# Graph attention by lists of edges: an index beyond a bound for edges of a later block

## The chip, the cores and the metric

The kernel runs on one core of a Trainium2 chip. The metric is the device time of one execution in microseconds (us): 4299.35 us, the median of three runs (4293.27, 4299.35 and 4299.38).

## What is computed

The program is a network of four graph layers and four feed-forward layers over 3125 nodes with 256 features and 50000 edges (src, dst), sorted by dst. The change touches the first two graph layers, which are graph attention with 4 heads of 64 features. Cut to what matters:

```
h = (x @ W.T).reshape(N, 4, 64)
e = leaky_relu(a_s[src] + a_d[dst], 0.2)          # one number per edge and head
m = segment_max(e, dst);  p = exp(e - m[dst])
alpha = p / (segment_sum(p, dst)[dst] + 1e-16)
out = segment_sum(alpha[:, :, None] * h[src], dst)
```

In the first layer every node also has an edge to itself. The other layers (mixtures of experts, a recurrence, graph convolutions, a dense form of the third attention) are not touched.

## The kernel before

**Blocks and places.** The nodes are cut into T = 25 blocks of P = 125. Since the edges are sorted by dst, the edges of a block are a run of the list. The list lies in HBM as a table (`k.EP`) with W = 17 edges to a row, four numbers to an edge: dst, two codes for another purpose, and src. Block b reads 128 rows of it, beginning at or just before its first edge (the number is in `k.at`), so partition p holds 17 successive edges, and a block has 128 x 17 = 2176 places. A block has 2000 edges in the mean. The places left over hold edges of the block before (fewer than two rows of them) and, mostly, edges of the block after. Places beyond the last edge hold -1.

**The edge loop.** `by_edges` runs once for each of the two layers (call them loop 1 and loop 2), 25 blocks each, and all engines work on several blocks at a time, in step by semaphores:

- SyncE loads the records of a block (`records`, L842) into one of six buffers `egs`.
- VectorE makes the indices, `indices(b)` at L894 to L899: src as an int32, not below 0, into one of three buffers `ids`. It first waits for the records and, from block 3 on, for the gathers of block b - 3, which read the same buffer.
- GpSimd (POOL in the profile) gathers, L826 to L834: for each of the 17 columns w one indirect DMA, which fetches for each of the 128 partitions the row of `k.HR` (264 floats: features with a one per head, and the source term of the score) that the index names. The rows land in one of four buffers `hgs`. It waits for the indices, and from block 4 on for the sums of block b - 4, which used the buffer last.
- VectorE, when the 17 gathers of block b have landed, copies the source terms for the list of maxima (`spread`, L947 and L948), and in later steps makes the maxima, the scores (`logits`) and the weights, and multiplies the gathered rows by them (`weigh`, L1008). Places whose dst is not in the block get weight 0, by the column of ones that their empty row of the one-hot matrix leaves out.
- TensorE sums the rows of a block by a matmul with the one-hot matrix of dst (L1156); ScalarE copies, widens and takes exponentials.

Beside this every second block, in each loop, also makes a block of a dense count matrix for the later layers (class `Adjacency`): VectorE at L545 and L556, TensorE at L619 and L630, ScalarE at L567, L580, L586 and L596.

**The order on VectorE** is written out by hand: step i holds maxima(i-2), sums(i-3), spread(i-1), indices(i+1), logits(i-2), the close of block i-3, the work for the count matrix, weigh(i-2) and hot(i). The indices of block i+1 are made right behind the spread of block i-1.

**The table** is written once, before loop 1, by class `EdgeTable`; L414 puts src into its fourth number, a conversion of 125 x 400 numbers.

Of the kernel before, what the change touches and what calls it, by code (L numbers as in the profile page):

```python
# [4 lines left out]
N, E, D = 3125, 50000, 256  # L5
P, T = 125, 25
# [2 lines left out]
TOL = 2.0 ** -18  # L9
EPS = 1e-5  # L10
W, FOLD, ROWE = 17, 782, 3070
SLOTS = 56
ROWS, LINE, LIST = 4 * W, 32 * 5, 96 * 5
GROUPS = [range(4 * g, min(4 * g + 4, T)) for g in range(7)]
# [2 lines left out]
ALU = mybir.AluOpType  # L17
# [107 lines left out]
def two_starts(e, out, src, sig):  # L125

    for lo, hi in ((0, 112), (112, P)):
        e.dma_start(out[lo:hi], src[lo:hi]).then_inc(*sig.by(16))  # L128


def indirect(ap):
    return bass.IndirectOffsetOnAxis(ap, 0)


def iota(e, out, pattern, base=0, up=0):
    return e.iota(out, pattern, base=base, channel_multiplier=up, allow_small_or_imprecise_dtypes=True)
# [171 lines left out]
class EdgeTable:  # L308
# [92 lines left out]
    def vector_first(self, e):  # L401

        vs, rec, sf, over = self.vs, self.rec, self.sf, self.over
        e.memset(self.next1[:, :], 1 << 20)
        e.memset(self.next63[:, :], -1).then_inc(*self.next_set.by())
        e.memset(self.pad[:, :], -1.0).then_inc(*self.pad_set.by())
        e.memset(self.tot[:, T:T + 1], float(E))
        e.memset(self.pos[:, T:T + 1], float(E))
        e.wait_ge(*self.dst_in.at(16))
        e.tensor_copy(self.df[:, :], self.de[:, :]).then_inc(*self.floats.by())  # L410
        e.tensor_copy(rec[:, :, 0], self.de[:, :])
        e.wait_ge(*self.src_in.at(16))
        e.tensor_copy(sf[:, :], self.se[:, :]).then_inc(*vs.by())
        e.tensor_copy(rec[:, :, 3], self.se[:, :])  # L414
        e.wait_ge(*self.numbered.at(1))
        e.wait_ge(*self.lasts.at(1))
        e.tensor_tensor(self.passed[:, :, :], self.k.PS[0:P, 4, 0:P].unsqueeze(1).broadcast_to([P, T, P]),
                        self.nodes[:, :].unsqueeze(2).broadcast_to([P, T, P]), ALU.is_lt).then_inc(*vs.by())
        e.wait_ge(*vs.now())
        e.tensor_reduce(self.row[:, :], self.passed[:, :, :], AX.X, ALU.add).then_inc(*vs.by())  # L420
        e.wait_ge(*vs.now())
        e.tensor_scalar(self.row[:, :], self.row[:, :], float(P - 1), None, ALU.min).then_inc(*vs.by())
        e.wait_ge(*vs.now())
        e.tensor_copy(self.rowi[:, :], self.row[:, :]).then_inc(*self.rows_set.by())
        for x in range(3):
            e.tensor_scalar(over[x][:, :], sf[:, :], float(FOLD * (x + 1)), None, ALU.is_ge).then_inc(*vs.by())
        for x in range(3):
            e.wait_ge(*vs.now())
            e.scalar_tensor_tensor(sf[:, :], over[x][:, :], -float(FOLD), sf[:, :], ALU.mult,
                                   ALU.add).then_inc(*vs.by())  # L430
        e.wait_ge(*vs.now())
        e.tensor_copy(rec[:, :, 1], sf[:, :]).then_inc(*vs.by())
        e.wait_ge(*vs.now())
        e.tensor_scalar(sf[:, :], over[0][:, :], 63.0, 1.0, ALU.mult, ALU.add).then_inc(*vs.by())
        e.wait_ge(*vs.now())
        e.scalar_tensor_tensor(sf[:, :], over[1][:, :], 4032.0, sf[:, :], ALU.mult, ALU.add).then_inc(*vs.by())
        e.wait_ge(*vs.now())
        e.scalar_tensor_tensor(rec[:, :, 2], over[2][:, :], 258048.0, sf[:, :], ALU.mult,
                               ALU.add).then_inc(*self.rec_set.by())
# [329 lines left out]
def by_edges(k, HA, SD, loops, close, odd):  # L769
# [10 lines left out]
    with ExitStack() as ctx:  # L780
        ioP, part = k.sb(ctx, [128, P], bf16), k.sb(ctx, [128, T])
        egs = [k.sb(ctx, [128, W, 4]) for _ in range(6)]
        id16 = k.sb(ctx, [128, 128], bf16)
        ids = [k.sb(ctx, [128, W], i32) for _ in range(3)]
        hgs = [k.sb(ctx, [128, W, 264]) for _ in range(4)]
        dts = [k.sb(ctx, [128, W, P], bf16) for _ in range(2)]
        wides = [k.sb(ctx, [128, W, P]) for _ in range(2)]
# [18 lines left out]
        eg_in, hg_in = k.sigs("eg_in", 6), k.softs("hg_in", 4)  # L806
# [3 lines left out]
        vs = k.sig("vstep")  # L810
        idx_made, dt_made, listed_out, sl_made = (
            k.sig(s) for s in ("idx_made", "dt_made", "listed_out", "sl_made"))
# [9 lines left out]
        with k.block() as block:  # L822
            @block.gpsimd
            def _(e):
                iota(e, ioP[:, :], [[1, P]]).then_inc(*numbered.by())
                iota(e, part[:, :], [[P, T]], up=1).then_inc(*numbered.by())  # L826
                adj.gpsimd(e)
                for i in range(T):
                    e.wait_ge(*idx_made.at(i + 1))
                    if i >= 4:  # L830
                        e.wait_ge(*summed.at(i - 3))
                    for w in range(W):
                        e.indirect_dma_start(hgs[i % 4][:, w, :], None, k.HR,  # L833
                                             indirect(ids[i % 3][:, w:w + 1])).then_inc(*hg_in[i % 4].by(16))  # L834

            @block.sync
            def _(e):
# [51 lines left out]
            def _(e):  # L889
# [4 lines left out]
                def indices(b):  # L894
                    e.wait_ge(*eg_in[b % 6].at(16 * (b // 6 + 1)))
                    if b >= 3:
                        e.wait_ge(*hg_in[(b - 3) % 4].at(16 * W * ((b - 3) // 4 + 1)))
                    e.tensor_scalar(ids[b % 3][:, :], egs[b % 6][:, :, 3], 0.0, None,
                                    ALU.max).then_inc(*idx_made.by())  # L899

                def maxima(b):
# [132 lines left out]

                e.wait_ge(*numbered.at(2))
                indices(0)
                for i in range(T + 4):
                    if i - 3 == adj.last:
# [7 lines left out]
                    if i + 1 < T:  # L1046
                        indices(i + 1)
# [225 lines left out]
class Counts:  # L1273

    SLOTS = [0, 7, 0, 7]

# [5 lines left out]
    def load(self, e, x, sig):  # L1284
        for n, t in enumerate(SETS[x]):
            two_starts(e, self.ADS[:, self.SLOTS[x] + n, :], self.k.ADJ16[t], sig)

    def of(self, x, j):
        return self.ADS[:, self.SLOTS[x]:self.SLOTS[x] + len(SETS[x]), j * P:j * P + P]

# [426 lines left out]
def attention_layer_one(k, HA, SD, bias):  # L1717
    with ExitStack() as ctx:
        close = CloseFirst(k, ctx, bias)

        def any_order():
            with ExitStack() as c:
                acc = k.sb(c, [P, T, 260])
                slow = AnyOrder(k, c)
                slow.degrees(k.deg)
                slow.attention(c, 4, 64, HA, SD, True, acc)
                close.signals(k)
                close_all(k, close, acc)

        for k.way in ways(k):  # L1730
            if k.way == "listed":
                by_edges(k, HA, SD, True, close, 0)
            else:
                any_order()
            k.over()
        k.way = "main"
# [16 lines left out]
def attention_layer_two(k, SD, H1):  # L1753

    with ExitStack() as ctx:
        close = CloseSecond(k, ctx, H1)

        def any_order():
            with ExitStack() as c:
                acc = k.sb(c, [P, T, 260])  # L1760
                slow, none = AnyOrder(k, c), k.sb(c, [P, N], f16)
                slow.attention(c, 4, 64, None, SD, False, acc)
                with k.block() as block:
                    @block.gpsimd
                    def _(e):
                        e.memset(none[:, :], 0.0)
                with k.block() as block:
                    @block.sync
                    def _(e):
                        for x in range(2):  # L1770
                            for t in SETS[x]:
                                e.dma_start(k.ADJ16[t], none[:, :]).then_inc(slow.landed, 16)
                        e.wait_ge(slow.landed, 16 * 13)
                slow.clear()
                close.signals(k)
                close_all(k, close, acc)

        either(k, lambda: by_edges(k, None, SD, False, close, 1), any_order)
# [1150 lines left out]
class Keep:  # L2929
# [5 lines left out]
    def __init__(self, k, ctx, hid, W1, W2, CC, scale):  # L2935
        self.k, self.hid, self.W1, self.W2, self.CC = k, hid, W1, W2, CC
        self.nh, self.width = hid // 128, hid // 128 + (4 if scale else 0)
        self.expert = k.sb(ctx, [128, SLOTS], i32)
        self.source, self.target = k.sb(ctx, [128, SLOTS], i32), k.sb(ctx, [128, SLOTS], i32)
        self.weight = [k.sb(ctx, [P, T]) for _ in range(2)]  # L2940
# [141 lines left out]
class Placed:  # L3082
# [4 lines left out]
    def __init__(self, k, ctx, keep, room, free):  # L3087
        self.k, self.keep, self.free = k, keep, free
        self.hot_r = room[0:P, 2816:6016].bitcast(bf16).rearrange("p (j r) -> p j r", r=128)
        self.hot_q = room[0:P, 0:2800].bitcast(bf16).rearrange("p (f j q) -> p f j q", f=2, q=SLOTS)  # L3090
        self.sel, self.tri = k.sb(ctx, [P, T, 8], bf16), k.sb(ctx, [P, P], bf16)
# [493 lines left out]
```

## Time and profile before

| what | us |
|---|---|
| median of three runs | 4299.35 |
| span of the profiled execution, first to last instruction | 4296.7 |
| GpSimd busy, whole span | 1298.0 |
| of it the gathers of the edge loops (L833, 850 of them) | 841.3 |
| VectorE busy, whole span | 2685.5 |
| TensorE busy, whole span | 3470.3 |

For the profiled execution no time beside its span is given; the span is 2.65 us below the median of the runs. Busy shares hold for the whole program; the change is in two stretches of it, from about 83 to 680 us and from about 990 to 1600 us, and these have to be read by themselves. In the rows, L833 is the gather (its call begins at L833 of the kernel), L898 makes the indices, L947 is the first instruction behind the wait for the gathered rows, and times are us from the start of the span unless marked ns.

### The profile page before, as it was taken

How to read it: one execution, taken by the hardware profiler on the slowest of the kernel's cores; microseconds unless marked ns; L12 is line 12 of the kernel's file. 1: busy time of each engine (PE TensorE's matmuls, PEld its weight loads, DVE VectorE, ACT ScalarE, POOL GpSimd, SP SyncE). 2: the span in 40 equal slices, each digit the busy share in tenths (PEclk: the TensorE clock that was granted, in tenths of full speed). 3: DMA queues.
4: the chain of work that ended last, by engine and by line, in shares of the span. 5: the costliest groups of instructions: out<-in, count | busy, mean ns of one | idle time of the engine just before them, and what ended most of it. 6: DMA issues, size and time to landing. Idle time of an engine off the chain costs nothing. (4 is left out here: it accounts for less than half of the span.)

```text
span 4296.7 us, 64001 instructions
## 1 busy us (share of the span) xinstructions
PE 3470.3 (81%) x22446; PEld 2907.5 (68%) x22446; DVE 2685.5 (63%) x6833; ACT 1617.5 (38%) x4188; POOL 1298.0 (30%) x1348
## 2 busy tenths in 40 slices
PE   4677774745777785998899999799997899959695
PEld 3565653644565665775788888755587799949695
DVE  6899996564888857884688888741134433353544
ACT  2344542213444444552566666621101233310131
POOL 6777761736777720000000000000000222200263
PEclk8777886977788887999999999999999899979898
DMA  5455552244555555320000000154555211163424
GB/s 157 135 152 154 144 147 96 95 108 134 145 145 158 143 153 154 89 65 15 1 1 1 1 1 1 19 125 125 125 152 171 89 37 38 33 145 103 147 72 128
DMA packets 200528, 419.56 MB, mean 98 GB/s; under 512 B 58688, under 2 KB 131535, under 8 KB 199716
## 3 DMA queue, kind: packets, MB, share of 16 engines
q1 hardware_dynamic: 139300, 251.73, 21.4%
q0 software_dynamic: 60928, 164.04, 13.4%
q8 instruction: 163, 2.67, 0.3%
q14 instruction: 137, 1.12, 0.1%
HBM read 331.25 MB, written 84.36 MB: 97 GB/s over the span
## 5 line engine op out<-in xcount | busy, mean ns | idle before, releaser
L833 POOL DMA_INDIRECT sb<-features,sb x850 | 841.3, 990 | 262.2 <-issue 258.7
L2002 PE MATMUL ps<-sb 128*128 128x125 f32 x5184 | 635.6, 279 | 71.2 <-DVE sb L2066 70.1
L2002 PEld LDWEIGHTS ps<-sb 128*128 128x128 f32 x5184 | 595.0, 192 | 111.8 <-DVE sb L2066 110.5
L3392 ACT ACTIVATE sb<-ps,sb 128x128 f32<-128x128 f32 x784 | 221.1, 377 | 542.6 <-PE ps L3318 542.6
L2033 ACT ACTIVATE sb<-ps 128x125 f32<-128x125 f32 x1296 | 330.6, 273 | 223.3 <-PE ps L2002 194.7
L1156 PE MATMUL ps<-sb 128*125 128x260 f32 x1700 | 388.4, 387 | 15.4 <-PEq L1154 15.2
L1156 PEld LDWEIGHTS ps<-sb 128*125 128x125 f32 x1700 | 320.5, 190 | 97.9 <-issue 45.5
L3318 PE MATMUL ps<-sb 128*128 128x128 f32 x3136 | 381.8, 277 | 1.8 <-DVE sb L3359 1.8
L3318 PEld LDWEIGHTS ps<-sb 128*128 128x128 f32 x3136 | 367.8, 194 | 2.4 <-DVE sb L3359 2.3
L3332 PE MATMUL ps<-sb 128*128 x1568 | 366.0, 379 | 0.0
L3332 PEld LDWEIGHTS ps<-sb 128*128 128x128 f32 x1568 | 285.2, 190 | 32.2 <-issue 0.3
L3295 POOL DMA_INDIRECT rows_y<-sb x168 | 192.3, 1145 | 374.8 <-DVE sb L3371 360.5
L619 PE MATMUL ps<-sb 128*125 128x392 bf16 x850 | 248.0, 475 | 63.3 <-PEq L617 61.8
L1376 PE MATMUL ps<-sb 125*125 125x257 f32 x1250 | 281.2, 387 | 18.4 <-DVE sb L1474 12.1
L1376 PEld LDWEIGHTS ps<-sb 125*125 125x125 f32 x1250 | 238.2, 192 | 59.5 <-issue 16.7
L2410 PE MATMUL ps<-sb 125*128 125x500 f16 (+1 forms) x1400 | 275.7, 352 | 0.0
L2430 PE MATMUL ps<-sb 125*125 125x256 f16 x2500 | 273.4, 273 | 0.0
L2430 PEld LDWEIGHTS ps<-sb 125*125 125x125 f16 x2500 | 273.1, 136 | 0.3
L619 PEld LDWEIGHTS ps<-sb 128*125 128x125 bf16 x850 | 166.8, 204 | 131.7 <-issue 70.5
L3352 DVE COPY sb<-sb 128x512 f32 (+2 forms) x168 | 134.3, 800 | 179.7 <-PE ps L3318 179.3
L1008 DVE TENSOR_TENSOR sb<-sb,ps 128x1560 f32<-128x1560 f32 x150 | 244.3, 1684 | 1.7
L3371 DVE TENSOR_TENSOR sb<-ps,sb 128x256 f32<-128x256 f32 x168 | 71.4, 425 | 266.1 <-PE ps L3332 266.1
(356 smaller groups left out, 5283.3 us busy)
## 6 DMA issues: line engine op xcount, KB each, us to landing
sb<-adj SPq DMA_DIRECT2D x125, 683.6 KB
neg<-sb SPq DMA_DIRECT2D x25, 683.6 KB
adj<-sb SPq DMA_DIRECT2D x25, 683.6 KB
sb<-neg SPq DMA_DIRECT2D x25, 683.6 KB
sb<-rows_y SPq DMA_DIRECT2D x30, 560.0 KB
sb<-in_L_ffn_W SPq DMA_DIRECT2D x16, 1024.0 KB
sb<-features,sb POOLq DMA_INDIRECT x850
sb<-adj SPq DMA_DIRECT2D x125, 79.3 KB
```

The costliest lines, as they stand in the source:

```text
L619: r = e.matmul(k.PS[0:P, 2 + x, 0:392], dt[:, w, :], self.hots[w % 4][:, 392 * x:392 * x + 392], start=w == 0, stop=w == W - 1)
L833: e.indirect_dma_start(hgs[i % 4][:, w, :], None, k.HR, indirect(ids[i % 3][:, w:w + 1])).then_inc(*hg_in[i % 4].by(16))
L1008: e.tensor_tensor(v, v, shares[:, w0:w1, :].unsqueeze(3).broadcast_to([128, w1 - w0, 4, 65]), ALU.mult).then_inc(scaled_token.sem, 1)
L1156: m = e.matmul(k.PS[0:P, 6, 0:260], wides[u % 2][:, w, :], hgs[u % 4][:, w, 0:260], start=w == 0, stop=w == W - 1)
L1376: m = e.matmul(k.PS[0:P, n, 0:257], work[u % 7][:, n * P:n * P + P], HA[:, j, 0:257], start=j == 0, stop=j == T - 1)
L2002: return e.matmul(sums(n, g)[:, 0, :], V[:, y, (4, 0, 5, 1, 2, 3)[g], :], self.old_h(n)[:, y, :], start=False, stop=y == 1, skip_group_che ...
L2033: e.activation(Gt[:, row, :], sums(n, g)[:, 0, :], ACT.Tanh if row >= 4 else ACT.Sigmoid).then_inc(acted, 1)
L2410: m = e.matmul(out, part[:, j, 128 * h:128 * h + 128], self.ads[:, first:first + len(ts), j * P:j * P + P], start=j == 0 and x == 0, stop= ...
L2430: m = e.matmul(self.k.PS[0:P, v % 2, 0:D], self.ads[:, self.slot(v), j * P:j * P + P], part[:, j, :], start=j == 0 and x == 0, stop=j == T ...
L3318: m = e.matmul(hidden(n, c), w1s[n % deep][:, x, c, :], xts[n % 2][:, x, :], start=x == 0, stop=x == 1)
L3332: m = e.matmul(k.PS[:, 5 + n % 2, 0:D], hts[n % 2][:, c, :], w2f[:, bass.ds(v * (nh * D) + c * D, D)], start=c == 0, stop=c == nh - 1)
L3392: m = e.activation(hts[n % 2][:, c, :], hidden(n, c), ACT.Gelu, bias=cons[n % 4][:, c:c + 1])
```

## The change

```diff
@@ -9,6 +9,7 @@
 W, FOLD, ROWE = 17, 782, 3070
+SKIP = 4096.0
 SLOTS = 56
@@ class EdgeTable, vector_first
         e.tensor_copy(sf[:, :], self.se[:, :]).then_inc(*vs.by())
-        e.tensor_copy(rec[:, :, 3], self.se[:, :])
+        e.tensor_scalar(rec[:, :, 3], self.se[:, :], 1.0 / SKIP, None, ALU.mult)
@@ by_edges
         ids = [k.sb(ctx, [128, W], i32) for _ in range(3)]
+        beyond = k.sb(ctx, [128, W])
@@ by_edges, gpsimd
                     for w in range(W):
                         e.indirect_dma_start(hgs[i % 4][:, w, :], None, k.HR,
-                                             indirect(ids[i % 3][:, w:w + 1])).then_inc(*hg_in[i % 4].by(16))
+                                             indirect(ids[i % 3][:, w:w + 1]), bounds_check=N - 1,
+                                             oob_is_err=False).then_inc(*hg_in[i % 4].by(16))
@@ by_edges, vector, indices(b)
                     if b >= 3:
                         e.wait_ge(*hg_in[(b - 3) % 4].at(16 * W * ((b - 3) // 4 + 1)))
-                    e.tensor_scalar(ids[b % 3][:, :], egs[b % 6][:, :, 3], 0.0, None,
+                    if b < 4:
+                        e.tensor_scalar(ids[b % 3][:, :], egs[b % 6][:, :, 3], SKIP, 0.0, ALU.mult,
+                                        ALU.max).then_inc(*idx_made.by())
+                        return
+                    e.scalar_tensor_tensor(beyond[:, :], egs[b % 6][:, :, 0], float((b + 1) * P),
+                                           egs[b % 6][:, :, 3], ALU.is_ge, ALU.add).then_inc(*vs.by())
+                    e.wait_ge(*vs.now())
+                    e.tensor_scalar(ids[b % 3][:, :], beyond[:, :], SKIP, 0.0, ALU.mult,
                                     ALU.max).then_inc(*idx_made.by())
```

The table now holds src / 4096. From block 4 on, a place whose dst is at or beyond the first node of the next block gets (1 + src / 4096) x 4096 = 4096 + src as its index, which is more than the bound 3124 that every gather now carries; all other places get src as before (3125 is below 4096, and these fractions are exact in float32). For an index beyond the bound the gather copies nothing, and the place keeps the row that the block four earlier left in the buffer; its weight is 0. The first four blocks of each loop, whose buffers hold nothing yet, gather all places, with the bound in the instruction too. Places beyond the last edge hold -1 and still gather row 0.

## Rows read from the trace of the kernel before

**Rows 1.** The page, busy tenths of GpSimd and VectorE in 40 slices of 107 us.
```profile
DVE  6899996564888857884688888741134433353544
...
POOL 6777761736777720000000000000000222200263
```
**Rows 2.** Busy time by stretch: the middle of loop 1 and of loop 2.
```profile
core 0: us, PE busy (x) PEld busy (x) DVE busy (x) ACT busy (x) POOL busy (x), PEclk, DMA share, GB/s
151.00:624.00 473.00, 370.51 (x2098) 285.70 (x2099) 427.57 (x1000) 227.02 (x350) 360.75 (x369) 0.80 0.53 149
1057.00:1523.00 466.00, 363.46 (x2113) 281.17 (x2112) 384.03 (x850) 203.83 (x285) 356.80 (x359) 0.81 0.53 152
```
**Rows 3.** The gathers (L833) in loop 1: ns min/median/max, first and last start, waits.
```profile
L833 POOL DMA_INDIRECT sb<-features,sb x425: 949/949/2507, 83.2 to 628.5; - x142
its engine sat idle before it (us, times) until:
  issue: 129.3, 424
  DVE sb L898: 1.7, 1
who waited for it (us, times):
  DVE sb L947: 1.1, 1
```
**Rows 4.** The gathers (L833) in loop 2, the same columns.
```profile
L833 POOL DMA_INDIRECT sb<-features,sb x425: 949/949/2173, 989.5 to 1542.3; - x142
...
  DVE sb L947: 56.1, 24
```
**Rows 5.** The spread's first copy (L947), loop 1, then loop 2.
```profile
L947 DVE COPY sb<-sb x25: 167/175/370, 118.1 to 647.7; 128x17 f32<-128x17 f32 x25
...
L947 DVE COPY sb<-sb x25: 174/182/301, 1014.2 to 1545.3; 128x17 f32<-128x17 f32 x25
```
**Rows 6.** GpSimd in order of time: start, duration, last two gathers of loop 1.
```profile
627.19 0.96 POOL L833 DMA_INDIRECT sb<-features,sb  x1 [0.30 <-issue]
628.46 0.95 POOL L833 DMA_INDIRECT sb<-features,sb  x1 [0.30 <-issue]
```
**Rows 7.** VectorE in order of time around the first wait of loop 2's last block.
```profile
1543.99 0.29 DVE L1261 TENSOR_SCALAR sb<-sb 125x256 f32<-125x256 f32 x1
1545.25 0.18 DVE L947 COPY sb<-sb 128x17 f32<-128x17 f32 x1 [0.97 <-DMA sb<-features,sb]
```
**Rows 8.** VectorE in order of time around the indices of block 3, loop 1.
```profile
129.30 0.37 DVE L947 COPY sb<-sb 128x17 f32<-128x17 f32 x1
129.38 0.31 DVE L948 COPY sb<-sb 128x68 f32<-128x68 f32 x1
129.49 0.23 DVE L898 TENSOR_SCALAR sb<-sb 128x17 int32<-128x17 f32 x1
129.56 0.31 DVE L983 COPY sb<-ps 128x153 f32<-128x153 f32 x1
129.91 0.67 DVE L986 TENSOR_TENSOR sb<-sb,ps 128x153 f32<-128x153 f32 x2
130.72 0.23 DVE L989 TENSOR_TENSOR sb<-sb 128x68 f32<-128x68 f32 x1
130.98 0.23 DVE L992 SCALAR_TENSOR_TENSOR sb<-sb 128x68 f32<-128x68 f32 x1
131.25 0.23 DVE L995 TENSOR_TENSOR sb<-sb 128x68 f32<-128x68 f32 x1
```
**Rows 9.** Small VectorE groups in the middle of loop 1: busy us, mean ns, idle before.
```profile
L898 DVE TENSOR_SCALAR sb<-sb 128x17 int32<-128x17 f32 x21 | 6.1, 291 | 0.0
...
L992 DVE SCALAR_TENSOR_TENSOR sb<-sb 128x68 f32<-128x68 f32 x21 | 4.8, 229 | 0.7
...
L954 DVE TENSOR_SCALAR ps<-sb 128x17 f32<-128x17 f32 x21 | 3.9, 185 | 0.0
```
**Rows 10.** Indirect DMAs elsewhere: gather and scatter of 128 rows, gather of 125.
```profile
L3290 POOL DMA_INDIRECT sb<-rows_x,sb x168: 945/973/1403, 756.3 to 4233.2; - x168
...
L3295 POOL DMA_INDIRECT rows_y<-sb x168: 968/992/1488, 765.9 to 4251.6; - x168
...
L381 POOL DMA_INDIRECT sb<-in_dst,sb x25: 1210/1214/1490, 16.8 to 53.7; - x25
```
**Rows 11.** The conversion of src in the table, and a multiplication of its shape.
```profile
L414 DVE CAST sb<-sb x1: 511/511/511, 8.9 to 8.9; 125x400 f32<-125x400 int32 x1
...
L434 DVE TENSOR_SCALAR sb<-sb 125x400 f32<-125x400 f32 x1 | 0.4, 369 | 0.0
```

## The prediction

> **What bounds the kernel now.** I read the page's slices first, to find where GpSimd works: its gathers fill two stretches, slices 0 to 5 and 9 to 14, and these are the two edge loops [rows 1]. The chain of waits on the page is of no use here, since it is followed only through the program's last stage. So I asked for each loop by itself: busy time by stretch, then the gather's own line with its waits, then the first VectorE instruction that needs gathered rows.
>
> GpSimd never pauses in either loop. Its 425 gathers wait for the indices once, 1.7 us, and otherwise follow each other with 129.3 / 424 = 0.305 us of issue between them; most take 0.949 us [rows 3]. From first to last start it is (628.5 - 83.2) / 424 = 1.286 us a gather in loop 1, 21.9 us a block, and (1542.3 - 989.5) / 424 = 1.304 us, 22.2 us a block, in loop 2 [rows 3, 4].
>
> Who waits for the gathers differs. In loop 1 VectorE waited for them once, for 1.1 us [rows 3]: from the spread of block 1 at 129.30 to that of block 24 at 647.7 it needs 22.5 us a block [rows 5, 8], a little more than GpSimd, so GpSimd runs ahead. The last gather ends at 628.46 + 0.95 = 629.4 [rows 6], and its block is spread at 647.7. In the middle of that loop VectorE is busy 427.6 of 473 us in 1000 instructions; the rest is 0.045 us an instruction, and no wait [rows 2]. Loop 1 is bound by VectorE, with GpSimd just behind it. In loop 2 VectorE waits at 24 of 25 blocks, 56.1 us in all, 2.3 us each [rows 4], and its step is (1545.3 - 1014.2) / 24 = 22.1 us, GpSimd's own [rows 5]. The last spread begins at 1545.25, about 1.95 us behind the end of the last gather (1542.33 + 0.95), which is its landing [rows 4, 7]. Loop 2 is bound by the making of gathers on GpSimd. In neither loop is it bytes: the DMA engines are 0.53 busy at about 150 GB/s in both [rows 2], and the one wait on gathered rows ends a constant landing behind the last issue.
>
> **The change part by part.**
>
> *Rows not copied.* A block has 2176 places for 2000 edges in the mean. The 176 over, less about 9 for the edges before, are of the next block: some 160 places, 7.4%, which is 9 to 10 of each gather's 128 rows. Blocks 0 to 3 gather all and the last block has no next one, so 20 blocks of each loop are cut. As bytes this is worth nothing: 20 x 160 x 1056 B = 3.4 MB in a loop that moves 150 GB/s in 550 us, and nobody waits for bandwidth.
>
> *The gather instruction.* What decides is the time per gather on GpSimd, with its issue; call its change d. The trace of before has no gather with a bound. The price from below, if the time went with the rows copied: 0.949 x 0.074 = 0.070 us less, in 20 x 17 = 340 gathers. From above I take the dearest indirect DMA of the trace: the gather of 125 rows at L381 takes 1.214 us against 0.949, so d up to +0.265, and that in all 425 gathers, since the bound is in each. The nearest row speaks against the lower end: 125 rows cost more than 128, and 128 rows of 1024 B cost 0.945 where 1056 B cost 0.949 [rows 3, 10]. The time is thus not one per row. A scatter, whose other side is the indexed one, costs 0.968 at the least [rows 10]. I take d = 0, within 0.01.
>
> A rule bears on the 125 rows. The Trainium skill, DMA: Bandwidth & Descriptors, section "Why a DMA increments its semaphore by 16 and not by 1", says that the generator spreads a DMA over the largest number of engines up to 16 that divides the count of partitions: 16 for 128, 5 for 125. By that the 128 rows are 8 for each engine and the 125 rows 25, and an estimate from the two rows is 0.265 / 17 = 0.016 us for each further row of an engine, with 0.82 us fixed. Since the rows left out lie side by side, most engines would still have their 8 and nothing would be saved; at most 0.016 x 340 = 5 us would be. No row here shows how the generator treats a row that it skips. The sum below does without this.
>
> *VectorE, in blocks 4 to 24 (21 of each loop).* One scalar_tensor_tensor of 128 x 17 is added, and the old instruction, same shape, now waits for it. A chain of such dependent instructions of 128 x 68 starts one each 0.26 us (130.72, 130.98, 131.25) [rows 8]. For 17 columns in place of 68 take off 0.229 - 0.185 = 0.04 [rows 9]; for this place in the order, where L898 takes 0.291 against 0.185 elsewhere, add up to 0.11 [rows 9]. So 0.20 to 0.35 us a block; I take 0.25. Behind it in the queue stand the logits, the close, the hot rows and the weighing, all of VectorE's step. In loop 1 that is the bound: 21 x 0.25 = +5.3 us (4.2 to 7.4). In loop 2 it lies in the 2.3 us of waiting for each block [rows 4]: nothing; uncovered it would be the same 5.3. The indices still come about 20 us before the gathers that use them, so GpSimd does not wait.
>
> *The table.* L414 becomes a multiplication. It took 0.51 us, and a multiplication of the shape 0.37 [rows 11]: within 0.2 us either way, taken as 0. The other edits (a small buffer, the factor in the instruction) issue nothing.
>
> *Sum.* The span was 4296.7 and the median of the runs 4299.35, so 2.65 us lie around it. 4296.7 + 5.3 (loop 1) + 425 x 0 (loop 2) = 4302.0 as a span, 4304.7 as a time.
>
> **Rivals.**
>
> *A dearer gather (slower).* If the generator compares each index and handles two kinds of row, d is above 0. In loop 2 every bit of it shows: 425 d. In loop 1 GpSimd has 647.7 - 629.4 - 1.95 = 16.3 us in hand, 21.6 with VectorE's extra: it decides from d = 0.05 on. With d = +0.1: 42.5 in loop 2, 42.5 - 16.3 = 26.2 in loop 1, time 4368. With d = +0.03: 12.8 + 5.3, time 4317. With the upper end, 0.265: 112.6 + 96.3, time 4508. For it: the generator's time is flat and deterministic, thus a fixed program, and a bound is something for it to do. Against: if indices are always compared with some bound, nothing is added.
>
> *A cheaper gather (faster).* If time does go with rows written, loop 2 loses 340 x 0.070 = 24 us; VectorE has 2.3 us a block there to follow 1.2. Loop 1, bound by VectorE, gains nothing and pays its 5.3: time 4299.35 - 24 + 5.3 = 4281. Against it stand the rows of L381; for it, that nothing but GpSimd bounds loop 2, so that any saving shows.
>
> *The change does not do what it says*: the bound is checked but the rows are copied or replaced all the same. That is the forecast's time, as the bytes don't matter.
>
> **How the numbers follow.** Forecast (d within 0.01): chance 0.42, own range 4299 to 4311 (4.2 to 7.4, and 4.3 either way). Dearer gather: 0.36. Cheaper: 0.22. Within 0.2% is within 8.6 us of 4299.35, about what a measurement here can tell. Nearly all of the forecast's case is inside it, and a little of its upper edge out: same 0.40, slower 0.38, faster 0.22. The range is 4280 to 4380: it takes in most of the cheap end, and the dear one to about d = +0.11; beyond it 0.08 are left above and 0.08 below.
>
> **What would show it.** Each step has its line: the median of the gathers (0.949 if I am right; 0.88 in the cut blocks for the cheap rival, more everywhere for the dear one) and the 0.305 us of issue; the last start of loop 2 less its first (552.8 us now); VectorE's waits for gathered rows, still about once in loop 1 and about 2 us a block in loop 2 (shorter by the 0.25); the step of loop 1, from 22.5 to 22.8 us; and the new instruction at the side of L898 with 0.2 us or so. GpSimd's busy time and the two loops' lengths decide between the cases. Wrong would be a forecast in which loop 2's step moves by more than 0.2 us a block either way, or in which loop 1 turns out to wait for gathers.

## The result, and the profile after

The changed kernel takes 4325.3 us (median of four runs, 4322.2 to 4329.2) against 4299.4 us (4293.3 to 4303.2): a ratio of 1.006, 95% interval 1.0048 to 1.0073, so it is slower by 26 us. A second job gave 4324.1 against 4299.1, ratio 1.0061 (1.0047 to 1.0075). Ratios compare executions that took their kernel's usual time; one of the eleven of compare_only (below) took 7247 us and is left out of its ratio. The profiled execution has a span of 4325.2 us against 4296.7. The forecast was 4304.7 with no change that can be told; the range, 4280 to 4380, holds the time. What happened is the rival of the dearer gather, near the low end of its prices.

The gathers of the changed kernel in loop 1 and then in loop 2; the columns are those of [rows 3, 4].
```profile
L835 POOLq MOVE  x425: 29/29/29, 82.8 to 634.4; - x142
L835 POOL DMA_INDIRECT sb<-features,sb x425: 994/999/2088, 83.6 to 650.9; - x142
its engine sat idle before it (us, times) until:
  issue: 129.3, 424
  DVE sb L902: 2.4, 1
who waited for it (us, times):
  DVE sb L957: 3.3, 3
...
L835 POOLq MOVE  x425: 29/29/37, 1001.7 to 1553.6; - x142
L835 POOL DMA_INDIRECT sb<-features,sb x425: 994/999/2989, 1002.5 to 1569.8; - x142
...
  DVE sb L957: 68.4, 25
```
The median gather has gone from 0.949 to 0.999 us, in both loops. The issue between gathers has not: 129.3 us in 424 gaps, 0.305 us each, as before, although GpSimd's sequencer now makes a register move of 29 ns ahead of each gather, which the trace of before did not have (the bound is given in a register). VectorE waits for gathers more: 3 times in loop 1, 25 times in loop 2, 68.4 us in place of 56.1 [rows 3, 4].

The same gathers as a group, with the mean: before, loop 1 and loop 2, then after, loop 1 and loop 2 (busy us, mean ns | idle before).
```profile
L833 POOL DMA_INDIRECT sb<-features,sb x425 | 416.9, 981 | 131.1 <-issue 129.3 <-DVE sb L898 1.7
...
L833 POOL DMA_INDIRECT sb<-features,sb x425 | 424.4, 999 | 131.1 <-issue 129.3 <-DVE sb L898 1.7
```
```profile
L835 POOL DMA_INDIRECT sb<-features,sb x425 | 439.0, 1033 | 131.7 <-issue 129.3 <-DVE sb L902 2.4
...
L835 POOL DMA_INDIRECT sb<-features,sb x425 | 439.1, 1033 | 131.6 <-issue 129.2 <-DVE sb L902 2.3
```
The mean rose by 0.052 us in loop 1, about as the median did, but in loop 2 by 0.034 only: there the gathers that take longer than the median cost less than before.

The spreads: the first copy in loop 1, the last spread of loop 2, and that of block 4 in loop 1. They answer to [rows 5, 7].
```profile
L957 DVE COPY sb<-sb x25: 169/173/188, 118.9 to 658.0; 128x17 f32<-128x17 f32 x25
...
1572.81 0.18 DVE L957 COPY sb<-sb 128x17 f32<-128x17 f32 x1 [1.00 <-DMA sb<-features,sb]
...
199.90 0.18 DVE L957 COPY sb<-sb 128x17 f32<-128x17 f32 x1 [0.67 <-DMA sb<-features,sb]
199.99 0.19 DVE L958 COPY sb<-sb 128x68 f32<-128x68 f32 x1
200.10 0.18 DVE L905 SCALAR_TENSOR_TENSOR sb<-sb 128x17 f32<-128x17 f32 x1
```
From these the 28.5 us between the two spans are placed. Loop 1's last spread is at 658.0 in place of 647.7: +10.3. From there to the first gather of loop 2 it is 344.5 us in place of 341.8: +2.7. Loop 2, first gather to last spread, takes 570.3 in place of 555.7: +14.6. Behind it, 2752.3 in place of 2751.4: +0.9. So 24.9 of the 28.5 us are in the two loops. The 2.7 between them, where no gather carries the bound, have no cause that is shown: the other kernels near 4300 us have 0.8 to 3.0 there.

Bytes did fall, as the change says. The GpSimd queue of the page, before and after (packets, MB, share):
```profile
q0 software_dynamic: 60928, 164.04, 13.4%
```
```profile
q0 software_dynamic: 60928, 156.94, 13.2%
```
These are 7.1 MB fewer, near the 2 x 3.4 of the estimate, in the same number of packets. What a left-out row turns into can be read from the packets' sizes in the traces. Before, each gather makes 32 packets of 4224 B, four rows of 1056 B each. After, 1948 of these 27200 are smaller: 3172, 2120, 1068 or 16 B, which is four rows with three, two, one or none of them whole and 4 B in place of each of the others. So a row beyond the bound keeps its place in its packet and is 4 B long. By this count 6744 rows are left out, 169 for each of 40 blocks, where the prediction had some 160.

### The profile page after: what moved, and what is told of

It reads as the page before. It is cut to its first block and busy times, and to the rows that moved or that the text cites. A ratio compares the mean times of both kernels' runs of the same rounds, so it can differ in the third digit from the quotient of the medians.

```text
span 4325.2 us, 64893 instructions
## 1 busy us (share of the span) xinstructions
PE 3474.3 (80%) x22446; PEld 2906.4 (67%) x22446; DVE 2694.2 (62%) x6875; ACT 1617.2 (37%) x4188; POOL 1334.3 (31%) x1348
## 5 line engine op out<-in xcount | busy, mean ns | idle before, releaser
L835 POOL DMA_INDIRECT sb<-features,sb x850 | 878.1, 1033 | 263.2 <-issue 258.5
```

The source lines that it names most:

```text
L835: e.indirect_dma_start(hgs[i % 4][:, w, :], None, k.HR, indirect(ids[i % 3][:, w:w + 1]), bounds_check=N - 1, oob_is_err=False).then_inc(* ...
```

## The experiments

Theory: a gather that carries a bound costs GpSimd a fixed 0.050 us more, whatever its indices. Rival 1: the price belongs to the rows left out. Rival 2: it belongs to VectorE's compare. A later rival: to the register move. "The bound" is always `bounds_check` together with `oob_is_err=False`; no run has one without the other, so which of them costs the time isn't shown. Ratios are to runs of the kernel before in the same job, which is one session on one chip in which both are timed.

**bound_only.** The kernel before, with one edit:
```diff
-    indirect(ids[i % 3][:, w:w + 1])).then_inc(*hg_in[i % 4].by(16))
+    indirect(ids[i % 3][:, w:w + 1]), bounds_check=N - 1,
+                            oob_is_err=False).then_inc(*hg_in[i % 4].by(16))
```


> The kernel before with the bound 3124 in every gather and nothing else: every index is within it, no row is left out, VectorE and the table are as before. Theory (a gather that carries a bound costs GpSimd a fixed 0.050 us more, whatever its indices): median gather 0.999 us from block 0 to block 24, last spread of loop 1 some 5 to 8 us later, loop 2 longer by 15 to 21 us, time 4320 to 4327 us. Rival 1 (the price is that of rows left out, or of telling two kinds of row apart): median 0.949 us, time 4299 us. Rival 2 (the time comes from the compare that VectorE makes ahead of the indices): median as it may be, time 4299 us.

Measured: 4319.9 us, ratio 1.0045 (1.0031 to 1.0059). The gathers in loop 1 and then loop 2:
```profile
L833 POOL DMA_INDIRECT sb<-features,sb x425: 994/1002/2137, 83.2 to 649.7; - x142
...
L833 POOL DMA_INDIRECT sb<-features,sb x425: 995/1002/2703, 999.8 to 1564.2; - x142
```
The median is 1.002 us with no row left out. Last spread of loop 1 at 655.0 (+7.3), loop 2 longer by 11.6 us from first gather to last spread (555.7 to 567.3; 15 to 21 were expected). The bound alone accounts for 18.3 of the 26 us. The loops' lengths are of one trace each. Rival 2 falls for most of the price, rival 1 for the price itself.

**compare_only.** The changed kernel, without the bound, and with:
```diff
-    e.scalar_tensor_tensor(beyond[:, :], egs[b % 6][:, :, 0], float((b + 1) * P),
+    e.scalar_tensor_tensor(beyond[:, :], egs[b % 6][:, :, 0], 1.0e9,
```


> The changed kernel without the bound in the gathers and with a threshold of 1e9 in the compare, so that every index is src as before: table factor, compare and dependent multiplication stay on VectorE. Theory: gathers 0.949 us, step of loop 1 longer by 0.25 to 0.31 us a block, last spread of loop 1 5 to 6.5 us later, nothing in loop 2, time 4304 to 4306 us. Rival 1: the same. Rival 2 (VectorE's extra pair is what costs): loop 2 longer too, time 4315 us or more.

Measured: 4302.8 us, ratio 1.0004 (0.9995 to 1.0014). Gathers and the spread's first copy, loop 1:
```profile
L835 POOL DMA_INDIRECT sb<-features,sb x425: 947/949/2594, 83.1 to 631.2; - x142
...
L956 DVE COPY sb<-sb x25: 169/174/290, 119.4 to 651.9; 128x17 f32<-128x17 f32 x25
```
The last spread of loop 1 is 4.2 us later (651.9 against 647.7), below the 5 to 6.5 that were expected: 0.2 us a block over 21 blocks. Of the 4.2 us 0.8 are there already at the spread of block 4 (196.6 against 195.8), when two of the 21 compares have run; the other 3.4 come with the 19 behind, 0.18 us each. Loop 2 is not longer but 5.1 us shorter (550.6 us in this trace against 555.7): its mean gather stands 0.038 us above the median in place of 0.050, and 425 x 0.012 is 5.1. As a time (4304 to 4306 were expected) it can't be told from nothing.

**all_beyond.** The changed kernel with the threshold at -10, so that blocks 4 to 24 gather nothing (but row 0 for the places beyond the last edge).

> The changed kernel with the compare true for every place, so that in blocks 4 to 24 every index is beyond the bound and the gathers copy nothing (the sums of those blocks are of old rows). Theory (fixed price for the bound): median gather 0.999 us in blocks 4 to 24 as in blocks 0 to 3, time within 5 us of the changed kernel's 4325. Rival 1a (the price grows with the rows left out: 0.050 us for some 9 of 128): 0.6 us more a gather in blocks 4 to 24, time beyond 4700 us. Rival 1b (a row left out saves its descriptor): a gather well under 0.949 us in blocks 4 to 24, loop 2 bound by VectorE, time under 4300 us.

Measured: 4319.4 us, ratio 1.0051 (1.0037 to 1.0065). The gathers of blocks from 4 on in loop 1 (none copies a row), those of blocks 0 to 3 (all rows copied), and the queue. Then the page's count of packets of all queues, before and in this run:
```profile
L835 POOL DMA_INDIRECT sb<-features,sb x321: 994/998/1272, 220.0 to 648.9; - x161
...
L835 POOL DMA_INDIRECT sb<-features,sb x65: 994/998/2412, 83.9 to 169.2; - x65
...
q0 software_dynamic: 60928, 68.14, 5.8%
```
```profile
DMA packets 200528, 419.56 MB, mean 98 GB/s; under 512 B 58688, under 2 KB 131535, under 8 KB 199716
```
```profile
DMA packets 200536, 323.72 MB, mean 75 GB/s; under 512 B 81468, under 2 KB 154315, under 8 KB 199716
```
0.998 us whether 128 rows are copied or none. 96 MB fewer move in as many packets: 22780 packets of 4224 B have become packets of 16 B, four rows of 4 B. Both forms of rival 1 fall: a left-out row still takes its place in a packet, and GpSimd's time per gather is the same. What does get shorter is the landing: in loop 2 the spread begins 1.2 us behind the end of its last gather in place of 1.9. The time is 5.9 us below the changed kernel's first result, a little more than the 5 expected, with ratios that overlap (1.0051 and 1.006). This row ends the question of the change's intent too: if leaving out all rows takes nothing off a gather, leaving out 7% cannot.

**one_instruction.** The changed kernel with the compare moved into the table:
```diff
+    e.tensor_scalar(self.blocks[:, :], self.df[:, :], 1.0 / P, 0.5 / P - 0.5, ALU.mult, ALU.add)
+    e.scalar_tensor_tensor(rec[:, :, 3], self.blocks[:, :], SKIP, sf[:, :], ALU.mult, ALU.add)
...
+    e.tensor_scalar(ids[b % 3][:, :], egs[b % 6][:, :, 3], -SKIP * b, 0.0, ALU.add, ALU.max)
```
Blocks 0 to 3, whose edit isn't shown, take two dependent instructions here for the one of the changed kernel.


> The changed kernel with 4096 x block(dst) + src in the table, so that blocks 4 to 24 make the index by one instruction on VectorE, as before the change, and the same rows are left out (a row of an earlier block now gathers row 0; two small instructions more in the table, once). Theory: gathers 0.999 us as in the changed kernel, loop 1 shorter than the changed kernel's by what the compare costs where VectorE binds, at most 6 us, loop 2 the same: 4319 to 4324 us. Rival 2 (the compare is what costs): back to about 4300 us.

Measured: 4325.1 us, ratio 1.0057 (1.0043 to 1.007); 4319 to 4324 were expected. Gathers 0.998 us, last spread of loop 1 at 657.0, in place of 658.0 and 656.4 in the two traces of the changed kernel. With the bound in, taking the compare off VectorE gives back a microsecond at most: GpSimd sets the step of loop 1 here (last gather at 652.9, VectorE waits for gathers in 9 blocks, 7.7 us).

**move_only and bound_once.** The kernel before, with a register move ahead of each gather and no bound; and with the bound, its register set once a loop:
```diff
+    e.reg_mov(spare, N - 1)              # move_only, ahead of each gather
...
+    e.reg_mov(bound, N - 1)              # bound_once, ahead of the loop; bounds_check=bound
```


> The kernel before with a register move of the constant 3124 on GpSimd's sequencer ahead of every gather, which carries no bound. In the changed kernel such a move of 29 ns stands before each gather. Theory (the 0.050 us are spent by the making of a gather that has a bound): median gather 0.949 us, issue 0.305 us, time as before. Rival (the move that loads the bound costs the time): the gather and its issue together 1.304 us at the median in place of 1.254.

> The bound alone, as in bound_only, but its register is set once for each loop and no move stands between the gathers. Theory (the making of a bounded gather): median 0.999 us still, issue 0.305 us, time 4316 to 4325 us. Rival (the move): median 0.949 us, time 4300 us.

In this job the kernel before took 4871 us (15 runs), for reasons outside the change (below), and each of the two versions ran once (4877.5 and 4829.3 us), so their times decide nothing and only the gathers' own durations are read. move_only, then bound_once:
```profile
L835 POOL DMA_INDIRECT sb<-features,sb x850: 944/946/2926, 83.0 to 2080.8; - x170
```
```profile
L835 POOL DMA_INDIRECT sb<-features,sb x850: 992/998/2693, 83.4 to 2029.2; - x170
```
The move costs the gather nothing; the bound costs its 0.052 us without the move. The issue is 0.305 us at the median in both. The rival of the move falls.

**fewer_partitions.** The kernel before with `n = 128 if i < 4 else 64 if i < 11 else 112 if i < 18 else 125` partitions in the gathers; the sums of blocks 4 to 24 are of old rows in part.

> The kernel before with gathers over the first 64 partitions in blocks 4 to 10, 112 in blocks 11 to 17 and 125 in blocks 18 to 24 (the rest of the buffer keeps old rows, so those sums are of old rows); no bound. It prices a gather by its number of rows. Theory of the prediction (a program with a large fixed part; 0.016 us for each further row of an engine, an estimate from 0.949 and 1.214 us): 0.89 us with 64 rows, 0.93 with 112, 1.2 with 125. Rival (the time goes with the rows): 0.47, 0.83 and 0.93 us.

It ran once, in a job in which the kernel before took 4894 us (4905.0 us), so the time decides nothing. The gathers of loop 1 in blocks of 128, 64, 112 and 125 partitions, in this order:
```profile
L834 POOL DMA_INDIRECT sb<-features,sb x63: 942/946/2120, 89.4 to 185.2; - x63
...
L834 POOL DMA_INDIRECT sb<-features,sb x110: 902/908/1218, 214.6 to 429.7; - x110
...
L834 POOL DMA_INDIRECT sb<-features,sb x108: 927/933/1326, 449.3 to 658.8; - x108
...
L834 POOL DMA_INDIRECT sb<-features,sb x117: 1191/1207/1467, 690.1 to 869.1; - x117
```
Half the rows save 0.038 us of 0.946, and three rows fewer than 128 cost 0.26 more. The reading of L381 in the prediction was right: the time of a gather does not go with its rows.

By the rule cited there (the Trainium skill, DMA: Bandwidth & Descriptors, "Why a DMA increments its semaphore by 16 and not by 1") these are 8, 4, 7 and 25 rows to an engine. The trace agrees, by its packets: 16 of four rows for a gather of 64 partitions, 16 of four and 16 of three for 112, 30 of four and 5 of one for 125, which is 5 times 25. The gathers of 125 also make 66 packets of 16 B and 11 of 4 B that those of 128 do not, as many as 11 times 25 words of 4 B. An estimate from the four medians is 0.008 to 0.015 us for each further row of an engine; whether the rows or the small packets cost the time, these rows can't tell.

**relu_on_scalar, relu_again, before_again, before_third.** The mean of loop 2 grew by less than the median. In the trace of before, 20 of the 22 gathers of loop 2 that overlapped VectorE's L1261 were among the long ones (1.18 us and more), in the changed kernel 13 of 22. So L1261, a maximum with 0, was put on ScalarE:
```diff
-        e.tensor_scalar(x, x, 0.0, None, ALU.max).then_inc(*vs.by())
...
+        e.wait_ge(*self.x_made.at(b + 1))
+        e.activation(x, x, ACT.Relu)
```


> The kernel before with the last step of loop 2's close, the maximum with 0 over 125 x 256 numbers (L1261), moved from VectorE to ScalarE. In the trace of before 20 of the 22 gathers of loop 2 that overlapped it took 1.18 us or more. Theory (that instruction holds up the gather beside it, and loop 2 is bound by gathers): some 20 long gathers fewer in loop 2, its mean gather down by 0.010 us, the loop shorter by 4 to 6 us, time 4294 to 4297 against 4300. Rival (long gathers fall there by chance or another instruction takes its place): the mean gather of loop 2 as before, no difference in time.

> The kernel before, unchanged, for a second trace: how far two executions of one kernel differ. In its first trace the mean gather of loop 2 stood 0.049 us above the median, in the four kernels with a bound 0.022 to 0.034, so that loop 2 grew by less than 425 x 0.050 = 21 us. If the excess belongs to the kernel (where VectorE's instructions fall), it is again 0.045 to 0.052; if it belongs to the execution, it is anywhere from 0.02 to 0.05.

> The same kernel as relu_on_scalar (loop 2's maximum with 0 on ScalarE in place of VectorE), once more, since in that job the kernel before itself took 4871 us, GpSimd waited for its indices in both loops and the gathers bound neither. Where loop 2 is bound by gathers (the kernel before near 4300 us): theory, mean gather of loop 2 down by 0.010 us, loop 2 shorter by 4 to 6 us, time 0.1% less; rival, no difference. Where it is not (near 4870 us): nothing can be told of the gathers, and the ratio should be 0.998 again.

> The kernel before, for a trace beside that of relu_again on the same chip. Where the kernel takes about 4300 us: mean gather of loop 2 0.045 to 0.052 us above the median if the excess belongs to the kernel; anywhere from 0.02 to 0.05 if it belongs to the execution.

These ran in jobs in which the kernel before took 4871 and 4894 us (4867.8 and 4895.5 in the two traced executions), so they do not answer the question. relu_on_scalar: 4862.6 us, ratio 0.9983 (0.9974 to 0.9992); relu_again: 4890.1 us, 0.9993 (0.9984 to 1.0002), where 0.998 was expected. The kernel before in the first of these jobs, its gathers:
```profile
L833 POOL DMA_INDIRECT sb<-features,sb x850: 944/946/3019, 83.5 to 2076.3; - x170
its engine sat idle before it (us, times) until:
  DVE sb L898: 522.1, 45
  issue: 245.4, 805
```
GpSimd waits 522 us for indices, so here no gather binds. The means of either loop stood 0.030 to 0.035 us above the median in the four traces. In the two of the kernel before, no gather of loop 2 overlaps L1261 at all. Whether loop 2 of the kernel before has its larger excess in every execution near 4300 us stays open: there is one such trace. compare_only, without a bound and near 4300 us too, has 0.038 there, and 7 of its 16 gathers beside that instruction are long, so the excess moves without a bound as well.

**after_again.** The changed kernel once more.

> The changed kernel itself, once more. Where the kernel before takes about 4300 us, the same ratio, 1.005 to 1.007, and a mean gather of loop 2 0.025 to 0.040 us above the median. Where the kernel before takes 4870 us or more, GpSimd waited 520 us for its indices over both loops and had the time for 850 x 0.050 = 43 us more: theory (a fixed price per gather, seen only where gathers bind), the gathers at 0.999 us and no increase in time, ratio 0.99 to 1.002. Rival (the price shows wherever the kernel runs): 1.004 or more.

Measured: ratio 1.0061 (1.0047 to 1.0075), given above. Median 0.998, mean gather of loop 2 0.032 us above it, last spread of loop 1 at 656.4: what the first trace showed. Whether the price vanishes where the kernel before takes 4870 us was thus not tried with this kernel. bound_once alone speaks to it, with a single execution: 4829 us where the kernel before took 4871, so no increase; why it is less, no run tells.

## Why the prediction was wrong in its likeliest case

**What bounds the loops: right.** That GpSimd binds loop 2 and is just behind VectorE in loop 1 is what made 0.050 us a gather show, and it is why the range reached far upwards.

**Rows and bytes: right.** The bytes fell about as worked out, and nothing came of it; all_beyond shows the same with nearly all rows left out.

**The gather: this is the step that failed.** "I take d = 0, within 0.01" rested on rows that show what the number and the size of rows cost. None of them has a bound, so they could speak against the cheaper gather, and did so rightly, but not for zero: the price of an added operand was unseen, and I let the evidence against one rival stand for the forecast. It measured +0.050 at the median (0.949 to 0.999, and 0.946 to 0.998 in another job), whatever the indices, in both loops; even the shortest gather went from 0.949 to 0.994. Of what makes the gathers only this is shown: the price depends neither on the rows left out nor on the move, and a row left out still has its place in a packet. Whether it is one price for a gather or a small one for each of its 128 indices isn't shown, since no run has the bound with fewer partitions. Both of the prediction's own signs of being wrong came: loop 2's step went from 22.1 to 22.7 us, and loop 1 waits for gathers at its start. That the time fell inside the range is owed to the rival, to which 0.36 was given, and not to the forecast.

**The rival's sum: right in total, less so in its parts.** With d = 0.05 its formula gives 21.3 in loop 2, nothing beyond the compare's 5.3 in loop 1, 26.6 in all: 4325.9 against 4325.3. Measured were 14.6 and 10.3 (and 2.7 between the loops, of which I know no cause; bound_only and after_again show about 3 as well). In loop 2 6.5 us came back, since the excess of the long gathers over the median fell from 425 x 0.050 = 21 us to 425 x 0.034 = 14.5. In loop 1 I counted GpSimd's advance as 16.3 us, which it has at the end. At block 1 it is 0.2 us by the same count (the spread begins 2.1 us behind the last gather's end, and 1.95 are the landing). So the gathers bind the first blocks: block 4 is spread at 199.9 in place of 195.8, behind a wait, and those 4.1 us are about the 85 x 0.050 of the gathers up to it. Block 4's spread before:
```profile
195.76 0.17 DVE L947 COPY sb<-sb 128x17 f32<-128x17 f32 x1
```
The other 6.1 us of the 10.3 come in the 20 blocks behind: there VectorE waits for no gathers (its three waits are at blocks 1, 2 and 4) and needs 22.9 us a block in place of 22.6, GpSimd 22.7. compare_only gives 3.4 of the 6.1 to the compare; for the other 2.7 no cause is shown. Slack that builds up in the course of a loop can't be spent at its start.

**VectorE's compare: right in kind, a little high.** 0.25 us a block was taken, from a range of 0.20 to 0.35; compare_only shows 4.2 / 21 = 0.20 over the whole loop, and 0.18 behind block 4. It did not add up with the bound: one_instruction takes it away for a microsecond at most, since the gathers, at 22.7 us a block, then hold VectorE up.

**The table, the indices in time: right.** GpSimd waited for indices once in each loop, at its first gather, as before.

No version here beats the kernel before near 4300 us. relu_on_scalar was faster by 0.17% in one of the two jobs near 4880 us, and in the other the difference can't be told from nothing; near 4300 us it was not run.

## What to carry to other kernels

Where a kernel is bound by the making of indirect DMAs, count gathers and their options, not bytes: in these runs a gather over 128 partitions cost 0.95 us and 0.30 us of issue, a bound in it added 5% to the 0.95, and with the bound it cost the same whether it copied 128 rows or none. A new operand on an instruction that binds a loop is a cost that no row of the trace bounds; give it a price above zero, multiplied by its count, even if its intent is to save work. And read an engine's advance over the next at the start of a loop, not at its end.

## What the runs showed of the hardware that I had not expected

A row beyond the bound is not dropped: it stays in its packet with 4 B in place of 1056, and saves GpSimd nothing.

A gather of 125 partitions takes 1.207 us where 128 take 0.946: for GpSimd three partitions more are cheaper than three fewer.

The same kernel took 4299 to 4302 us in three jobs and 4871 and 4894 us in two others. Where the record names the chip, it is another one in each job: 4 and 10 for the short times, 13 and 11 for the long ones. Nearly all of the difference is in the edge loops: what follows the last spread took 2751.4, 2748.7 and 2753.8 us. The median gather there is as short (0.946), yet a block of loop 1 takes 32.7 us in place of 22.6, with pauses on TensorE that no other engine's record explains. In this one of 7.2 us, in the kernel before (before_again), VectorE and ScalarE stand idle too, 3.6 and 6.3 us up to 630.6 and 630.7, and the profile names nothing that released them:
```profile
622.31 0.51 PE L630 MATMUL ps<-sb 125*125 125x125 bf16 x6
623.38 0.21 PE L630 MATMUL ps<-sb 125*125 125x125 bf16 x1 [0.56 <-issue]
624.09 0.21 PE L630 MATMUL ps<-sb 125*125 125x125 bf16 x1 [0.50 <-issue]
631.51 2.73 PE L630 MATMUL ps<-sb 125*125 125x125 bf16 x15 [7.21 <-PEq L628]
```
The cause was not tried. TensorE's granted clock is lower in the loops there, 0.68 and 0.70 in place of 0.79, but its busy time grew by 38 and 28 us only, where the loops grew by 278 and 266. It means that which engine binds these loops, and so what a bound costs, is not the same wherever the kernel runs.
